# Norms of a convolution and a mixer in four groups of 14 rows over two PSUM banks

## The reference: what is computed

```
def _L1_conv_ref(x, ln_w, ln_b, w_in, b_in, conv_w, conv_b):
    mu = mean(x, -1); var = mean((x - mu)**2, -1)
    h = (x - mu) * rsqrt(var + LN_EPS) * ln_w + ln_b
    xz = einsum('bhwc,cd->bhwd', h, w_in) + b_in
    x1, z = split(xz, 2, -1)
    y = conv_3x3_same(x1, conv_w) + conv_b
    return x + silu(y)

x = _L0_conv_ref(x, ...)            # window attention and MLP
x = _L1_conv_ref(x, ...)            # the convolution block
t = tokens(x)
t = t + _L2_attn_ref(_ln_t(t), ...) # norm, then Fourier mixer 0
t = t + _L2_ffn_ref(_ln_t(t), ...)
t = t + _L3_attn_ref(_ln_t(t), ...) # norm, then Fourier mixer 1
t = t + _L3_ffn_ref(_ln_t(t), ...)
```

## Time and profile before

| | us |
|---|---|
| median of 3 runs | 3586.49 |
| lowest and highest run | 3586.38 and 3595.33 |
| the profiled execution | 3582.79 |
| its span, first to last instruction | 3581.0 |

### The profile page before, as it was taken

How to read it: one execution, slowest core, us unless ns; L and a number is a source line. 1 busy time by engine, 2 the same in 40 slices (tenths; PEclk the granted TensorE clock), 3 DMA queues, 4 the chain that set the end, 5 groups by cost and what they waited for, 6 DMA issues and landing times.

```text
span 3581.0 us, 110301 instructions
## 1 busy us (share of the span) xinstructions
PE 3136.2 (88%) x48876; PEld 1960.8 (55%) x48876; DVE 1810.5 (51%) x2898; ACT 1649.4 (46%) x3027; POOL 215.5 (6%) x462
## 2 busy tenths in 40 slices
PE   6978889888898898988989889898898988898888
PEld 3536646367455574554745647546465474564744
DVE  5425555355643546445564455634456355563555
ACT  3553354533555425554355443453544535445344
POOL 4510000000000000000000000000000000000000
PEclk9999999999999999999999999999999999999999
DMA  2321000110011100110001100011000110001100
GB/s 78 66 52 45 2 16 4 49 31 2 16 25 36 23 2 16 32 39 12 2 16 32 49 2 2 17 50 31 2 2 17 49 31 1 2 17 32 31 1 15
DMA packets 31253, 84.83 MB, mean 24 GB/s; under 512 B 24818, under 2 KB 25954, under 8 KB 26930
## 3 DMA queue, kind: packets, MB, share of 16 engines
q1 hardware_dynamic: 29506, 72.56, 8.5%
q0 software_dynamic: 1280, 5.21, 0.5%
HBM read 61.70 MB, written 14.84 MB: 21 GB/s over the span
## 4 chain that ended last, share of the span: by engine, by line
PE 73%; ACT 11%; DVE 6%; issue 4%; SPq 4%; DMA 2%; ACTq 0%; DVEq 0%
PE ps L1097 73%; ACT rs L698 3%; ACT lv L693 3%; DVE area_ty L918 2%; SPq L488 2%; DMA area_hz<-f_all 1%; DMA area_ty<-area_hz 1%; DVE xs L1066 1%; SPq L503 1%; ACT area_ty L779 1%; ACT area_ty L785 1%; DVE area_ty L1062 1%; DVE area_ty L1038 0%; ACT sq L685 0%; DVE area_ty L1007 0%
## 5 line engine op out<-in xcount | busy, mean ns | idle before, releaser
L918 DVE TENSOR_TENSOR area_ty<-ps,rs 128x448 f32<-128x448 f32 (+2 forms) x416 | 285.2, 686 | 470.1 <-ACT rs L698 470.1
L1097 PE MATMUL ps<-area_hz 32*64 32x147 f32 (+2 forms) x7180 | 364.0, 289 | 91.7 <-DVE area_hz L956 33.6
L1097 PE MATMUL ps<-area_ty,area_hz 113*64 113x49 f32 (+1 forms) x10240 | 393.1, 249 | 19.2 <-DMA area_ty<-area_hz 16.4
L1097 PEld LDWEIGHTS ps<-area_hz 32*64 32x64 f32 (+2 forms) x7180 | 292.6, 156 | 196.9 <-issue 172.9
L803 ACT ACTIVATE area_hz<-ps 121x384 f32<-121x384 f32 (+2 forms) x256 | 129.6, 519 | 577.6 <-PE ps L1097 577.6
L1097 PE MATMUL ps<-sq,keep_sb 64*64 64x448 f32 (+1 forms) x1664 | 368.2, 536 | 30.1 <-ACT sq L685 23.3
L1097 PEld LDWEIGHTS ps<-area_ty,area_hz 113*64 113x64 f32 (+1 forms) x10240 | 331.6, 135 | 101.6 <-issue 101.3
L693 ACT ACTIVATE lv<-ps 128x448 f32<-128x448 f32 (+1 forms) x416 | 217.8, 523 | 314.9 <-PE ps L1097 312.7
L939 DVE TENSOR_REDUCE area_hz<-ps 113x12 f32<-113x588 f32 x256 | 196.4, 769 | 275.2 <-PE ps L1097 274.6
L1097 PE MATMUL ps<-area_ty,g_sb 56*112 56x192 f32 (+1 forms) x3712 | 311.4, 321 | 26.0 <-DVE area_ty L1038 19.7
L1097 PE MATMUL ps<-xs,keep_sb 64*64 64x448 f32 x1120 | 262.7, 556 | 63.1 <-DVE xs L1066 31.4
(11 more groups left out here) (114 smaller groups left out, 3885.9 us busy)
## 6 DMA issues: line engine op xcount, KB each, us to landing
area_hz<-f_all SPq DMA_DIRECT2D x16, 2541.0 KB
xw<-x_in SPq DMA_DIRECT2D x8, 1568.0 KB, 6.6
y_out<-xs SPq DMA_DIRECT2D x32, 252.0 KB
f_all<-piece POOLq DMA_DIRECT2D x16, 317.6 KB, 3.6
area_ty<-area_hz SPq DMA_DIRECT2D x256, 4.6 KB
area_hz<-raw_in SPq DMA_DIRECT2D x1, 2894.0 KB, 9.6
g_sb<-g_in SPq DMA_DIRECT2D x6, 355.2 KB
g_sb<-g_in SPq DMA_DIRECT2D x2, 710.5 KB
```

Of the source, the lines that this page charges most:

```text
L918: ve.tensor_tensor(o, a, b, ALU.mult, **kw).then_inc(normed, 1)
L1097: return pe.matmul(o, a, b, start=start, stop=stop)
```

## The change

The convolution's norm and mixer 0's norm go in four groups of 14 rows (`NP`, `PR`, `PT` = 784 columns) in place of seven tiles of 8. Group i owns banks 2i and 2i+1 (`pair_banks`). Centering and variance of a group are four 64 x 64 products of 392 columns, one for each half of the images and each half of the columns; Square, Ln and Exp of a group are one ACT instruction over 784 elements. The scale multiplies `xs` itself, not the centered tile, by `rs`; the centering matrix is multiplied into `wconv` and `mix1` in the set-up instead, with two products and two DVE copies. The convolution's groups are 28 rows each, so chunks are 7 rows and 392 columns in both. The order on TensorE is written anew, the filler products between the mixer's centerings and its variance 0 are gone, and those ahead of mixer 0 are put behind the wait for the first scaled group.

```
-GROUPS, GROUP_AT = 2, [0, 4 * TR]
+GROUPS, GROUP_AT = 2, [0, HW // 2]
 CHUNKS = 4
-CR = [TR, (HW - 4 * TR) // CHUNKS]
+CR = [HW // 2 // CHUNKS] * 2
+NP = 4
+PR = HW // NP
+PT = PR * HW
+PH = PT // 2
...
 # ACT
+                if in_pairs(which):
+                    act.activation(halves(sq[:, k % 2, :]), pair_banks(i), ACT.Square).then_inc(squared, 1)
+                    return
...
-                for i in range(NT):
-                    if i + 1 < NT:
+                for i in range(NP):
+                    if i + 1 < NP:
                         square(q, LN_CONV, i + 1)
                     invert(q, LN_CONV, i)
...
 # DVE
+            def scale_pair(q, which, i, o):
+                k = LN_AT[which, i]
+                ve.wait_ge(root, ln_count(q, k))
+                a, b = (v.rearrange("p (h w) -> p h w", w=HW)
+                        for v in (xs[:, PT * i:PT * i + PT], rs[:, k % 2, :]))
+                ve.tensor_tensor(o, a, b, ALU.mult).then_inc(normed, 1)
...
+            ve.wait_ge(su_pe, 8)
+            su(ve.tensor_copy(wconv[:, :, :], ps[:, 0, 0:9 * RW].rearrange("p (t n) -> p t n", t=9)))
+            su(ve.tensor_copy(mix1[:, :, :], ps[:, 1, 0:2 * QI * CI].rearrange("p (l n) -> p l n", l=2)))
...
 # TensorE
+                mm(ps[:, 0, 0:9 * RW], K("center"), wconv.rearrange("p t n -> p (t n)")).then_inc(su_pe, 1)
+                mm(ps[:, 1, 0:2 * QI * CI], K("center"), mix1.rearrange("p l n -> p (l n)")).then_inc(su_pe, 1)
...
+                def center_pair(which, i):
+                    for p in range(2):
+                        r = slice(64 * p, 64 * p + 64)
+                        for c in range(2):
+                            at = PT * i + PH * c
+                            ins = mm(ps[64 * c:64 * c + 64, 2 * i + p, 0:PH], K("center")[r, r], xs[r, at:at + PH])
+                    ins.then_inc(centered, 1)
+                def variance_pair(which, i):
+                    k = LN_AT[which, i]
+                    pe.wait_ge(squared, ln_count(q, k))
+                    for c in range(2):
+                        r = slice(64 * c, 64 * c + 64)
+                        for p in range(2):
+                            ins = mm(ps[64 * p:64 * p + 64, 2 * i + c, 0:PH], K("variance")[r, r],
+                                     sq[r, k % 2, PH * p:PH * p + PH])
+                    ins.then_inc(var_made, 1)
...
                 def center_mix(i):
-                    pe.wait_ge(conv_added, q * GROUPS * CHUNKS + chunks_under(i))
-                    center(q, LN_MIX(0), i, xs)
+                    pe.wait_ge(conv_added, q * GROUPS * CHUNKS + max(CHUNKS, 2 * i + 2))
+                    center_pair(LN_MIX(0), i)
...
                 center_conv(0)
                 center_conv(1)
+                variance_pair(LN_CONV, 0)
+                center_conv(2)
+                variance_pair(LN_CONV, 1)
                 pe.wait_ge(mlp_added, q * NW + NW)
-                center_conv(2)
-                variance(q, LN_CONV, 0)
-                for i in range(3, 6):
-                    variance(q, LN_CONV, i - 2)
-                    center_conv(i)
-                variance(q, LN_CONV, 4)
+                center_conv(3)
                 pe.wait_ge(border, q + 1)
-                pe.wait_ge(normed, ln_count(q, LN_AT[LN_CONV, 3]))
+                pe.wait_ge(normed, ln_count(q, LN_AT[LN_CONV, 1]))
                 tap(0, 0)
-                center_conv(6)
+                variance_pair(LN_CONV, 2)
                 tap(0, 1)
-                variance(q, LN_CONV, 5)
                 tap(0, 2)
-                variance(q, LN_CONV, 6)
+                variance_pair(LN_CONV, 3)
                 for n in range(3, 9):
                     if n == 6:
-                        pe.wait_ge(normed, ln_count(q, LN_AT[LN_CONV, 4]))
+                        pe.wait_ge(normed, ln_count(q, LN_AT[LN_CONV, 2]))
                     ins = tap(0, n)
...
                 center_mix(0)
                 center_mix(1)
+                variance_pair(LN_MIX(0), 0)
+                move(1)
+                variance_pair(LN_MIX(0), 1)
                 center_mix(2)
-                pe.wait_ge(conv_added, q * GROUPS * CHUNKS + CHUNKS)
-                keep_busy(3, 2)
-                variance_mix(0)
-                move(1)
-                for i in range(1, NT):
-                    variance_mix(i)
-                    if i + 2 < NT:
-                        center_mix(i + 2)
+                center_mix(3)
+                variance_pair(LN_MIX(0), 2)
+                variance_pair(LN_MIX(0), 3)
...
-                keep_busy(5, 2)
-                pe.wait_ge(normed, ln_count(q, LN_AT[LN_MIX(l), NT - 1]))
+                if l == 0:
+                    pe.wait_ge(normed, ln_count(q, LN_AT[LN_MIX(0), 0]))
+                keep_busy(5 if l else 1, 2)
+                pe.wait_ge(normed, ln_count(q, LN_AT[LN_MIX(l), NT - 1 if l else NP - 1]))
```

More of the change, by code:

```diff
@@ L101, in chunk_rows @@
     return slice(HW * at, HW * (at + CR[g]))
[L104 to L108, removed]
 FFN_SLOTS = NT + 3
+NP = 4
+PR = HW // NP
+PT = PR * HW
+PH = PT // 2
 def _tile_order():
-    order = [(LN_WIN2, i) for i in range(NW)] + [(LN_CONV, 0), (LN_CONV, 1)]
-    order += [(LN_CONV, i) for i in range(2, NT)] + [(LN_MIX(0), i) for i in range(NT)]
+    order = [(LN_WIN2, i) for i in range(NW)]
+    order += [(LN_CONV, i) for i in range(NP)] + [(LN_MIX(0), i) for i in range(NP)]
     for l in range(2):
@@ L141, in ln_width, with in_pairs @@
     return TW if which in (LN_FIRST, LN_WIN1, LN_WIN2) else TT
+def in_pairs(which):
+    return which in (LN_CONV, LN_MIX(0))
 def two_before(k):
@@ L154, in center_bank @@
         return 6
[L155 to L158, removed]
+    assert not in_pairs(which)
     return {LN_MIX(1): 1, LN_WIN1: 1}.get(which, 0)
@@ L165, in variance_bank @@
         return 2 + i % 2
-    if which == LN_MIX(0):
-        return 3 if i < CHUNKS else i + 1
-    if which in (LN_WIN2, LN_CONV):
+    assert not in_pairs(which)
+    if which == LN_WIN2:
         return 7
@@ L173, in user_before @@
 def user_before(bank, k):
-    same = [j for j in range(0 if k >= 0 else -NW, k) if bank(j) == bank(k)]
+    same = [j for j in range(0 if k >= 0 else -NW, k)
+            if not (j >= 0 and in_pairs(LN_ORDER[j][0])) and bank(j) == bank(k)]
     return same[-1] if same else None
@@ L183, in rows_needed @@
 def rows_needed(i):
-    rows = {(h - SHIFT) % HW // WS for h in range(TR * i, TR * i + TR)}
+    rows = {(h - SHIFT) % HW // WS for h in range(PR * i, PR * i + PR)}
     return max(MLP_ORDER.index(w) for w in rows) + 1
@@ L288, in build_kernel @@
         act_bias = sb("act_bias", [128, 2])
-        sq = sb("sq", [128, 2, TT])
-        lv = sb("lv", [128, 2, TT])
-        rs = sb("rs", [128, 2, TT])
+        sq = sb("sq", [128, 2, PT])
+        lv = sb("lv", [128, 2, PT])
+        rs = sb("rs", [128, 2, PT])
         wq = sb("wq", [128, 128])
@@ L432, in build_kernel, with pair_banks, halves @@
         block = ctx.enter_context(nc.Block())
+        def pair_banks(i):
+            return ps[:, 2 * i:2 * i + 2, 0:PH]
+        def halves(v):
+            return v.rearrange("p (c n) -> p c n", n=PH)
         @block.sync
@@ L692, in invert @@
                 act.wait_ge(var_made, ln_count(q, k))
-                act.activation(lv[:, k % 2, 0:w], ps[:, variance_bank(k), 0:w], ACT.Ln
-                               ).then_inc(logged, 1)
+                if in_pairs(which):
+                    w = PT
+                    act.activation(halves(lv[:, k % 2, :]), pair_banks(i), ACT.Ln).then_inc(logged, 1)
+                else:
+                    act.activation(lv[:, k % 2, 0:w], ps[:, variance_bank(k), 0:w], ACT.Ln
+                                   ).then_inc(logged, 1)
                 if two_before(k):
@@ L918, in scale, with scale_first @@
                 ve.tensor_tensor(o, a, b, ALU.mult, **kw).then_inc(normed, 1)
+            def scale_pair(q, which, i, o):
[4 more added lines that the diff above has]
+                ve.tensor_tensor(o, a, b, ALU.mult).then_inc(normed, 1)
             def scale_conv(q, i):
-                scale(q, LN_CONV, i, pad[:, 1 + TR * i:1 + TR * i + TR, 1:1 + HW])
+                scale_pair(q, LN_CONV, i, pad[:, 1 + PR * i:1 + PR * (i + 1), 1:1 + HW])
+            def scale_first(q, i):
+                scale_pair(q, LN_MIX(0), i,
+                           xhc[:, :, PR * i:PR * (i + 1)].rearrange("p w h -> p h w"))
             def scale_windows(q, which, i):
@@ L1013, in conv @@
                                          ).then_inc(conv_added, 1)
-                        if g == 1 and c == 1:
-                            scale_mix(q, 0, 0)
-                for i in range(1, NT):
-                    scale_mix(q, 0, i)
+                for i in range(NP):
+                    scale_first(q, i)
             def mixer(q, l):
```

10 lines of the change are left out of this document (4 added, 6 removed).

## The result

The changed kernel took 3573.96 us in the median (3566.53 to 3580.5), the kernel before beside it 3590.38; the ratio is 0.9948 (95%: 0.9935 to 0.9961), a gain of 18.7 us. The mean of both ratios, 0.9957, is 15.6 us; 27.7 were forecast. The time lies in the range and the sign is right, but it is above the forecast's own 3547 to 3569, and little more than half of the gain came. Of the 15 us between 3559 and 3573.96, 4 are the kernel before, which took 3590.38 here and 3586.5 when the forecast was made.

What follows compares the result with a forecast made beforehand. TensorE carried 73% of the chain. Seven quads at 6.45 gave 45.2 us, plus 4.2 of recovered half clock, less 21.7 of new half clock: 27.7 off the median 3586.5, so 3559 us; range 3537 to 3577.

Steps and rivals of the forecast that it cites:

- A: Convolution's norm, first centering to first tap: 10.7 us before, 8.1 computed, gain 2.6 a quad.
- B: First tap to first Exp of convolution group 0: 11.6 us before, 9.65 computed, gain 1.9 a quad.
- C: First Exp of convolution group 0 to `move(0)`: 7.0 us before, 6.1 computed, gain 0.9 a quad.
- D: `move(0)` to first Exp of convolution group 1: 3.6 us before, loss of 0.2 a quad computed.
- E: First Exp of group 1 to first Square of the mixer's norm: 4.2 us before, 4.9 computed, loss 0.7.
- F: First Square of the mixer's norm to mixer 0's first product: 15.4 us before, 13.0 computed, gain 2.4.
- the clock holds: Rival: the new gaps on TensorE cost no half clock, gain 45.2 + 4.2, 3537 us; chance 0.17.
- tiles on the same rows take turns: Rival: a paired centering or variance on TensorE costs 1.31 us, total gain 13, 3573 us; chance 0.11.
- The clock's term: Half clock behind TensorE's new idle gaps in the stage costs 3.1 us a quad, 21.7 in seven.
- First: Gap of 3.6 us ahead of the first tap: halves the clock in four quads of five, costs 1.1.
- Second: Gap of 4.3 us ahead of variance 0 of the mixer's norm: nearly always halves the clock, costs 1.4 at least.
- Third: Gap of 2.5 us ahead of mixer 0: taken together with the gap before it at 2.0 a quad.

Runs made afterwards that it cites:

- e1: Changed kernel with filler products in all three gaps (ahead of first tap, of the mixer norm's variance 0, of mixer 0): 3535.75 us, ratio to before 0.9861.
- after: The changed kernel itself, first profile, against the kernel before: 3573.96 us, ratio 0.9948.
- e2: Changed kernel with four filler products ahead of the first tap only: 3559.89 us, ratio to the kernel before 0.9926.
- e9: The changed kernel unaltered, run and profiled a second time beside the kernel before: 3572.68 us, ratio 0.9965.
- e3: Changed kernel with five filler products ahead of variance 0 of the mixer's norm only: 3555.13 us, ratio to the kernel before 0.9911.
- e4: Changed kernel with five instead of two filler products ahead of mixer 0 only: 3556.70 us, ratio to the kernel before 0.9917.

## Why the prediction was right, and where it was off

**At full clock the steps hold to a microsecond.** Sum 45.5 a quad at pairs of 0.65, and 45.6 in quad 1 of e1. Piece by piece (forecast, e1): A 8.1, 8.0; B 9.65, 9.85; C 6.1, 6.3; D 3.8, 3.9; E 4.9, 4.8; F 13.0, 12.9. The seven stages fell from 371.2 to 320.8, 50.4 us; 45.2 + 4.2 = 49.4 were computed. The rival "the clock holds" gave 3537 us, and with the gaps filled the kernel took 3535.75. That the totals agree so well is partly luck: at the pair price that was measured the sum would have been 53, but quad 5 of before, from which 52.5 was read, is 0.2 us longer than the other undisturbed quads, and the seven stages of e1 hold some 2 us over seven times 45.6, in quads without a drop.

**The price of a pair** was the one unknown with bounds, 0.65 to 0.87, and I took 0.75. In the rows, centering and variance of consecutive pairs start 0.66 us apart at full clock (2404.40, 2405.05, 2405.71 in quad 5): all four tiles run beside each other with no overhead. The lower end was right, the tap row misled me, and 0.55 us a quad, 3.9 in all, was left out of the sum. The rival "tiles on the same rows take turns" needed 1.31 and falls.

**ACT and DVE** were right to 0.05 us, and the rival of 0.95 us for Square and Ln falls. The Trainium skill's rule (TensorEngine Tiling, "PSUM Bottleneck"), that packed tiles leave the reading of PSUM as it was, gave 3.3 us a quad. The stages gave 7.2, or 6.7 between quads without a drop (52.3 and 45.6). In e1, ACT is busy 6.61 of 8.00 us in A and 9.62 of 12.90 in F, against 7.96 of 10.70 and 11.01 of 15.40 in the earlier trace rows. So of the 5.2 us that A and F lost, 2.7 are ACT's busy time, the rule's term, and 2.5 are idle time of ACT that went with the old ring; B, TensorE's own work, adds 1.8.

**The clock's term is the one that was mis-sized**: 3.1 us a quad, 21.7 in seven, were forecast; filling the gaps (e1) gave back 34 us by the ratios and 29 to 32 by the stretches (stage and mixer 0 of after, 870.8 and 868.4, less e1's 839.0), 4.2 to 4.9 a quad. By gaps:
- First: 1.1 a quad, in four quads of five. Measured: five of seven, and 7.5 us of stage in e2, 1.1 a quad. Read from piece B alone, against 9.82 us without a drop, it is 1.5 a quad in after and 1.4 in e9, since the drop lasted 6.8 us rather than 3.4 in five of these ten quads. Somewhat low.
- Second: 1.4 of the 2.0. Measured: seven of seven, 10.4 us of stage in e3, 1.5 a quad. Right.
- Third: the 0.6 that was left of the 2.0. Measured: the first group of mixer 0's products took 8.3 us more in seven quads, 1.2 a quad, and the filler of e4 took all of it away. This part was mis-sized by half. I priced the third gap as part of the norm, which ends there, and never costed what runs behind it at half clock: mixer 0's first products (the earlier trace rows end with them). The gap isn't new, either: before has one of 0.64 us at the same place (its row stands above), behind which the clock never dropped in seven quads. It is 2.35 us now, largely because the last Ln, Exp and scale take 0.82 + 0.86 + 1.55 = 3.2 us for 784 columns, where 448 took 0.54 + 0.58 + 0.93 = 2.05.

That makes about 4 us a quad for the three gaps, 28 in seven, more than half of what the stages gain at full clock. The other 5 to 7 us of mixer 0 have no cause from these runs. The group of products that starts 43 us into it takes 12.15 us when nothing disturbs it. Over seven quads it took 9.4 and 7.5 us more in after and e9, but also 6.0 more in e1 with all gaps filled, 2.5 in e4, 6.4 in e3 and 2.3 in before. A late drop of the clock, for 3.4 us, accounts for 1.55 us in each quad that has one; the rest stands in quads without one. So e4's 514.8 us against 530.0 and 528.0 overstates what the third gap costs.

```profile
2433.48 9.46 PE L1124 MATMUL ps<-mix,area_ty 64*64 64x96 f32 x224
```

This is e4's row of the first group of products in quad 5: 9.46 us as in before, and no gap in brackets.

**The Trainium skill's rule on the clock** (TensorE: Matmul & The Clock Gate, "Why this matters for your kernels") gave 3.4 a quad, 3561 us, by a cost in every quad for two gaps. The runs are on its side in the main, and beyond it, with some 4 a quad for three: e1 and e4 show what gaps cost between bursts, and that fillers remove it. But a gap of 3.35 us ahead of the first tap passed without a drop in quads 1 and 7 of after, and with one in the others.

**Quad 0** gained nothing, as said. Its table is issued at 232.72 us (230.77 before); the wait grew from 18.3 to 20.6, not to the 22 named, because the stage of quad 0 gained only 2.2 us, at half clock for 13.6 of its 50. In e1 the stage gains 6.75 and the wait is 25.6. The set-up cost nothing to be seen at the first keys (44.11 against 43.94 in the earlier trace rows).

**The sign**: slower would have taken 13 us of half clock over work bound by TensorE in a quad. Measured were 71.7 us behind the three gaps in seven quads, some 10 in each, and much of that over the mixer's norm, where ACT is busy for most of the piece (9.62 of 12.90 us in e1): the point wasn't reached.

## What to carry to other kernels

A change that takes work off TensorE must be costed with the gaps that it opens and the clock that can fall in them, and each gap with the work that runs behind it, in the next stage too; here filler products in three gaps brought back twice what the change had gained by itself. When a stage is computed piece by piece at full clock, make the run in which the clock holds: it separates a wrong step from a wrong clock. And before a transfer is moved forward on its queue, look at which other transfers something waits for at that time.

## What the runs showed of the hardware that I had not expected

- Four 64 x 64 products of 392 columns side by side are followed by the next four after 0.66 us, 1.67 ns a column (the rows at 2404.40, 2405.05 and 2405.71): no overhead, while a tap of sixteen 32 x 32 products of 392 columns takes 0.88 to the variance behind it in e1, 0.23 over its columns.
- Drops of the granted clock at these gaps lasted 3.4 us or 6.8 us. Behind the first gap, in after and e9, 6.8 us cost 2.5 to 2.9 us and 3.4 us cost 1.4 to 1.6 (piece B takes 9.82 us without a drop).
- A gap of only 2.35 us, the third, dropped the clock in five quads of seven, and one of 0.64 to 0.71 us, in before, in none.
- The same gap of 3.35 us dropped the clock in five quads of seven and not in two, in both profiles; what decides it, these runs don't show.
- DVE's scale of 784 elements costs 0.98 us into rows of the padded image and 1.55 into the mixer's layout, from the same two sources.
